# A new hand-written stream order and a new order of the first loads, in a one-core kernel of four transformer-like layers

## The chip, the cores and the metric

The kernel runs on one core of one Trainium2 chip. The metric is the device time of one execution in microseconds (us), from three runs. All arithmetic is float32. TensorE (PE in the rows) does the matrix products and transposes, VectorE (DVE) and ScalarE (ACT) move and transform what it leaves in its result banks, GpSimd (POOL) does small work for the normalisations and the residual sums, and SyncE (SP) issues every transfer between the chip's memory and the core.

## The reference, cut to what matters

There are 128 batch elements of 64 tokens with 128 features, a condition vector for each element, and a context of 64 tokens for each. Four layers follow each other:

```
layer 0:  x = x + g_sa * attend(ln(x)*(1+sc_sa)+sh_sa)        self attention, 16 heads of 8
          x = x + attend(ln(x), context)                       cross attention
          x = x + g_ff * mlp(ln(x)*(1+sc_ff)+sh_ff)            128 -> 512 -> 128, gelu
layer 1:  x = x + attend(ada_ln(x), ada_ln(context))
layer 2:  as layer 0, with ln(context) as its keys and values
layer 3:  x = x + g * out(sum_e p_e * expert_e([ln(x), evidence(x, context), anchor]))
```

The shifts, scales and gates (`sh`, `sc`, `g`) are products of silu(condition) with weights, so nothing that is modulated can start before the first modulation weights have landed.

## The kernel before, in words

The 128 elements are cut into 32 groups of 4 elements (256 tokens). A group runs through 91 named steps: `load`, `stats` (mean and variance), `normal` (normalised rows), `cols` (their transpose), `q`, `k`, `v`, `tops` (scores for the row maximum), `lows`, `scores`, `values`, `out`, `fc1`, `fc2`, the `l3_...` steps and `store`. Six streams, 0 to 5, each work through five or six groups, one after another; a stream's steps are in order, and each stream has its own tiles (`x_rows0`, `q_heads3`).

How the six streams are mixed is written out by hand in the string `SEQUENCE` (line 181): each digit is the next step of that stream, and each `f` the next of 18 set-up steps (`FOLDS`), which compute modulations, the gate rows and products of weights. `HALVES` says which half of TensorE's eight result banks each `tops` and `scores` takes. All engines walk the same list `ORDER` and each executes in that order what belongs to it, so **an instruction that waits holds up everything behind it on its engine**, whatever its stream. The string is periodic: from step 225 on, 546 steps (one group of each stream) repeat four times, before a tail of 503 steps. I call these parts the head, the four periods and the tail.

One normalisation goes through four engines: DVE sums up (`stats`, lines 1113 and 1116), POOL makes the reciprocal root (lines 707, 709, 711), DVE normalises the first 128 rows (line 1121) and ACT the other 128 (line 1279), and PE transposes (line 753).

`BY_START` lists the streams by the place of their first `stats`, and the SP program loads rows in that order. A list of weights, 12 transfers in all, is loaded with one shared semaphore `weights_in`; the only instruction that waits for it is the fold `("turn", 0)` on PE (the first transposes of line 800), and everything later on PE stands behind that. The gate rows are computed, stored to memory (`gate_store`, line 628) and loaded again for each stream, spread over the partitions (line 591). SP waits for the store to land before it goes on. The rows of streams 4 and 5 are loaded after that.

## Time and profile before

| what | value |
|---|---|
| median of 3 runs (lowest to highest) | 1828.96 us (1826.38 to 1832.3) |
| the profiled execution: its own time | 1832.71 us |
| its span, first to last instruction | 1830.8 us |
| PE busy | 1751.3 us, 96% of the span |
| DVE busy | 1554.5 us, 85% |
| ACT busy | 1484.3 us, 81% |
| POOL busy | 717.2 us, 39% |

The profiled execution took 1.9 us more than its span, and it stands 3.75 us above the median of the other runs. "Busy" is the union of an engine's instructions; an engine that is not busy waited either for another or for its own next instruction ("issue").

### The profile page before, as it was taken

How to read it: one execution, taken by the hardware profiler on the slowest of the kernel's cores; microseconds unless marked ns; L12 is line 12 of the kernel's file. 1: busy time of each engine (PE TensorE's matmuls, PEld its weight loads, DVE VectorE, ACT ScalarE, POOL GpSimd, SP SyncE). 2: the span in 40 equal slices, each digit the busy share in tenths (PEclk: the TensorE clock that was granted, in tenths of full speed). 3: DMA queues.
4: the chain of work that ended last, by engine and by line, in shares of the span. 5: the costliest groups of instructions: out<-in, count | busy, mean ns of one | idle time of the engine just before them, and what ended most of it. 6: DMA issues, size and time to landing. Idle time of an engine off the chain costs nothing.

```text
span 1830.8 us, 88396 instructions
## 1 busy us (share of the span) xinstructions
PE 1751.3 (96%) x38181; PEld 1503.1 (82%) x38181; DVE 1554.5 (85%) x3982; ACT 1484.3 (81%) x3598; POOL 717.2 (39%) x1401
## 2 busy tenths in 40 slices
PE   6889999999999999999999999999999999999998
PEld 5767788888888888888888888888888888878887
DVE  6868898888889888888988888988898898899765
ACT  4666897888888888888897888889888887786886
POOL 5323443343343344434344343434443444343341
PEclk9989999999999999999999999999999999999999
DMA  6000000000000000000000000000000000100000
GB/s 223 3 14 9 18 23 23 15 12 23 23 24 24 17 15 18 23 23 23 22 5 23 23 23 23 24 9 17 23 23 23 23 15 12 29 9 15 3 6 16
DMA packets 57841, 42.12 MB, mean 23 GB/s; under 512 B 13553, under 2 KB 56177, under 8 KB 57329
## 3 DMA queue, kind: packets, MB, share of 16 engines
q1 hardware_dynamic: 57456, 36.46, 6.8%
q8 instruction: 306, 5.01, 1.2%
q14 instruction: 79, 0.64, 0.1%
HBM read 31.99 MB, written 4.46 MB: 20 GB/s over the span
## 4 chain that ended last, share of the span: by engine, by line
PE 83%; DVE 8%; ACT 5%; issue 3%; DMA 1%; SPq 1%; DVEq 0%
PE half L1004 10%; PE half L902 8%; PE half L880 8%; PE half L921 8%; PE half L906 7%; PE half L939 6%; PE half L949 6%; PE half L1013 4%; PE half L753 4%; PE half L932 4%; PE half L867 4%; PE half L852 4%; PE half L856 3%; DVE top L1150 3%; ACT pT L1319 1%
## 5 line engine op out<-in xcount | busy, mean ns | idle before, releaser
L1150 DVE TENSOR_REDUCE top<-half 128x32 f32<-128x2048 f32 x160 | 364.5, 2278 | 48.8 <-PE half L880 47.7
L707 POOL TENSOR_TENSOR shifted<-moments,eps 128x2 f32<-128x2 f32 x256 | 50.5, 197 | 906.6 <-DVE moments L1116 906.3
L1319 ACT ACTIVATE pT<-half 128x512 f32<-128x512 f32 x640 | 330.0, 607 | 76.0 <-PE half L906 74.9
L902 PE MATMUL half<-o_rows,of_keys 32*128 32x128 f32 x5120 | 277.2, 282 | 7.8 <-issue 4.8
L906 PE MATMUL half<-q_heads,k_heads 32*128 32x128 f32 x5120 | 262.9, 271 | 0.0
L902 PEld LDWEIGHTS half<-o_rows,of_keys 32*128 32x128 f32 x5120 | 208.5, 186 | 31.1 <-issue 18.7
L1354 ACT ACTIVATE pT<-half,mod 128x64 f32<-128x64 f32 x896 | 196.5, 337 | 26.9 <-PE half L1004 25.8
L906 PEld LDWEIGHTS half<-q_heads,k_heads 32*128 32x128 f32 x5120 | 209.9, 187 | 0.1
L880 PE MATMUL half<-k_heads,q_heads 32*128 32x128 f32 x5120 | 188.0, 281 | 5.4 <-issue 2.0
L709 POOL TENSOR_TENSOR rstd<-shifted,minus_halves 128x2 f32<-128x2 f32 x256 | 182.8, 714 | 20.1
L880 PEld LDWEIGHTS half<-k_heads,q_heads 32*128 32x128 f32 x5120 | 160.4, 186 | 33.0 <-issue 15.5
L921 PE MATMUL half<-pT,v_cols 128*32 128x64 f32 x10240 | 177.7, 220 | 9.2 <-ACT pT L1319 4.6
L921 PEld LDWEIGHTS half<-pT,v_cols 128*32 128x32 f32 x10240 | 153.3, 110 | 38.7 <-issue 31.9
L1295 ACT ACTIVATE k_heads<-half,key_bias,own_head_sb 128x256 f32<-128x256 f32 x320 | 164.3, 573 | 24.3 <-PE half L856 22.7
L1142 DVE TENSOR_SCALAR q_heads<-half,b_sb,own_head_sb 128x256 f32<-128x256 f32 x320 | 156.7, 534 | 24.4 <-PE half L852 23.6
L1279 ACT ACTIVATE n_rows<-x_rows,minus,rstd 128x128 f32<-128x128 f32 x256 | 127.4, 504 | 29.6 <-POOL minus L711 27.6
L1113 DVE BATCH_NORM_STATS2 stats<-x_rows 128x6 f32<-128x128 f32 x512 | 122.4, 281 | 21.5 <-DMA x_rows<-x 18.4
L1303 ACT ACTIVATE v_cols<-half 64x256 f32<-64x256 f32 x320 | 122.7, 383 | 20.6 <-PE half L867 17.6
L1004 PE MATMUL half<-nT,w_sb 128*128 128x256 f32 x448 | 137.1, 387 | 2.1 <-issue 2.1
L939 PE MATMUL half<-nT,w_sb 128*128 128x256 f32 x512 | 133.3, 391 | 1.1 <-DVE top L1150 0.8
L1004 PE MATMUL half<-pT,w_sb 128*128 128x256 f32 x448 | 133.2, 379 | 0.7 <-issue 0.7
L949 PE MATMUL half<-w_sb,pT 128*128 128x128 f32 x1024 | 127.5, 277 | 1.0 <-DVE top L1150 0.6
(150 smaller groups left out, 3908.5 us busy)
## 6 DMA issues: line engine op xcount, KB each, us to landing
gates<-gate_store SPq DMA_DIRECT2D x128, 128.0 KB, 3.1
x_rows<-x SPq DMA_DIRECT2D x32, 128.0 KB, 2.8
c_rows<-context SPq DMA_DIRECT2D x32, 128.0 KB, 2.4
out<-n_rows SPq DMA_DIRECT2D x32, 128.0 KB, 1.9
w_sb<-weights SPq DMA_DIRECT2D x1, 1856.0 KB, 10.1
w_sb<-weights SPq DMA_DIRECT2D x2, 512.0 KB, 7.5
logit_bias<-logit_store SPq DMA_DIRECT2D x64, 1.5 KB, 3.5
row_sb<-rows SPq DMA_DIRECT2D x1, 769.5 KB, 7.7
```

The source lines that it names most:

```text
L709: nc.gpsimd.tensor_tensor(rstd[s][:, :], shifted[s][:, :], minus_halves[:, 0, :], ALU.pow).then_inc(rstd_in[s], 1)
L880: mm = nc.tensor.matmul(halves[HALF_OF[n]][:, g, tb * D:(tb + 1) * D], q_heads[s][part, tb, :, :], k_heads[s][part, tb, :, :], start=True, ...
L902: nc.tensor.matmul(halves[HALF_OF[n]][:, g, tb * D:(tb + 1) * D], of_keys[part, 2 * tb:2 * tb + 2, :], low[s][part, :], start=True, stop=F ...
L906: mm = nc.tensor.matmul(halves[HALF_OF[n]][:, g, tb * D:(tb + 1) * D], k_heads[s][part, tb, :, :], q_heads[s][part, tb, :, :], start=False ...
L921: mm = nc.tensor.matmul(dst[QUAD * g:QUAD * (g + 1), tb, :, lo, :], v_cols[s][:, at:at + QUAD], pT[s][:, g, tb, lo, :].rearrange("p (h q) ...
L939: mm = nc.tensor.matmul(dst[:, c * TOK:(c + 1) * TOK], w(layer["w1"], 0, 2 * half + c), nT[s][:, :, :], start=True, stop=True)
L949: mm = nc.tensor.matmul(dst[:, t * D:(t + 1) * D], hidden[s][:, c, t * D:(t + 1) * D], w(arg["w2"], c), start=c == 0, stop=c == 3)
L1004: mm = nc.tensor.matmul(dst[:, r * TOK:(r + 1) * TOK], weight, src[:, :, :], start=c == 0, stop=c == 1)
L1150: nc.vector.tensor_reduce(top[s][:, :].rearrange("p (g c) -> p g c", c=32)[:, :, 0:2 * GROUP], halves[HALF_OF[n]][:, :, :].rearrange("p g ...
L1295: m = nc.scalar.activation(k_heads[s][:, :, pair, :], bank4(src), ACT.Identity, scale=own_head[:, pair:pair + 1], bias=key_bias[:, n_att, ...
L1319: nc.scalar.activation(turn_cols[s][:, g, :], halves[HALF_OF[n]][:, g, :], ACT.Exp, scale=ATT_SCALE).then_inc(scores_read, 1)
L1354: m = nc.scalar.activation(dst, src[:, at], ACT.Silu, bias=mod[s][:, k, tb:tb + 1])
```

## The change

Two things change, and nothing that is computed. `SEQUENCE` and `HALVES` are other strings of the same length and with the same steps, again with a repeated block of 546 steps; the streams now begin in the order 2, 0, 1, 3, 4, 5. And the SP program loads the `x` rows of the first three streams directly behind the first modulation weights, splits the loads of `x` and `context` rows, and issues the 12 transfers of `weights_in` after the gates have been stored and loaded.

```diff
 SEQUENCE = (
-    "f023101200f0f11100f02104312f10102f31303120f23021f00023f04312f01420f11201f40310f32300f22104f22031f020"
+    "f2102012200f0f20023f01012210f23014f2311430f42102f01031f02022f10022f30231f23310f40231f11043f00240f413"
...
-                def load_rows(s):
+                def load_x(s):
                     sp.dma_start(x_rows[s][:, :, :], rows_of(x, s, 0)).then_inc(x_in[s], 16)
+
+                def load_context(s):
                     sp.dma_start(c_rows[s][:, :, :], rows_of(context, s, 0)).then_inc(c_in[s], 16)
...
                 load_weights(W_LOADS[0], 0, MOD_L0_COLS, mod_weights_in)
-                load_rows(BY_START[0])
+                for s in BY_START[:3]:
+                    load_x(s)
+                load_context(BY_START[0])
                 load_weights(W_LOADS[1], 0, L0_COLS, l0_weights_in)
+                for s in BY_START[1:3]:
+                    load_context(s)
                 load_weights(W_LOADS[0], MOD_L0_COLS, W_LOADS[0][3] - MOD_L0_COLS, later_mods_in)
-                load_rows(BY_START[1])
...
-                load_rows(BY_START[2])
-                load_weights(W_LOADS[1], L0_COLS, W_LOADS[1][3] - L0_COLS, weights_in)
-                for load in W_LOADS[2:]:
-                    load_weights(load, 0, load[3], weights_in)
-                load_rows(BY_START[3])
+                load_x(BY_START[3])
+                load_context(BY_START[3])
...
                 for s in BY_START[:4]:
                     load_gates(s, 0, 0)
+                load_weights(W_LOADS[1], L0_COLS, W_LOADS[1][3] - L0_COLS, weights_in)
+                for load in W_LOADS[2:]:
+                    load_weights(load, 0, load[3], weights_in)
                 for s in BY_START[4:]:
-                    load_rows(s)
+                    load_x(s)
+                    load_context(s)
                     load_gates(s, 0, 0)
```

The first place is the start of SP's queue, before. `pT5` and `pT4` are tiles of later streams that hold weights during set-up; the first holds the modulation weights, and `w_sb` with 1024 columns is the first layer's attention weights.

```order
L607 DMA pT5<-weights 128x768
L602 DMA x_rows0<-x 128x2x128
L603 DMA c_rows0<-context 128x2x128
L607 DMA w_sb<-weights 128x1024
L607 DMA pT5<-weights 128x1280
L602 DMA x_rows1<-x 128x2x128
L603 DMA c_rows1<-context 128x2x128
L619 DMA gates5<-rows 128x4x128
L620 DMA row_sb<-rows 128x1539
L602 DMA x_rows2<-x 128x2x128
L603 DMA c_rows2<-context 128x2x128
L607 DMA w_sb<-weights 128x3712
```

The same place in the changed kernel, and then the rows around the large weights.

```order
L609 DMA pT5<-weights 128x768
L602 DMA x_rows2<-x 128x2x128
L602 DMA x_rows0<-x 128x2x128
L602 DMA x_rows1<-x 128x2x128
L605 DMA c_rows2<-context 128x2x128
L609 DMA w_sb<-weights 128x1024
L605 DMA c_rows0<-context 128x2x128
L605 DMA c_rows1<-context 128x2x128
L609 DMA pT5<-weights 128x1280
```

```order
L630 DMA gate_store<-pT3 128x512
L591 DMA gates2<-gate_store 64x2x256 x2
L591 DMA gates0<-gate_store 64x2x256 x2
L591 DMA gates1<-gate_store 64x2x256 x2
L591 DMA gates3<-gate_store 64x2x256 x2
L609 DMA w_sb<-weights 128x3712
```

Three loads of `x` now stand together ahead of 1024 and 1280 columns of weights, and the large weights stand behind the gate store and eight gate loads; `x_rows4` follows behind all of them.

The second place is PE's queue around the first fold `turn` (the rows that transpose `w_sb` and `pT4`), before.

```order
L902 MATMUL half1<-o_rows1,of_keys 128x128 x4
L906 MATMUL half1<-q_heads1,k_heads1 128x128 x4
L852 MATMUL half0<-nT2,w_sb 128x256
L932 MATMUL half0<-w_sb,kvT0 128x128 x2
L800 MATMUL half0<-ident_sb,w_sb 128x128
L800 MATMUL half0<-ident_sb,pT4 128x128 x2
```

And in the changed kernel:

```order
L873 MATMUL half0<-w_sb,nT1 32x64 x16
L759 MATMUL half0<-ident_sb,c_rows3 128x128 x2
L927 MATMUL half0<-pT0,v_cols0 32x2x32 x32
L806 MATMUL half0<-ident_sb,w_sb 128x128
L806 MATMUL half0<-ident_sb,pT4 128x128 x2
L806 MATMUL half0<-ident_sb,w_sb 128x128
L908 MATMUL half1<-o_rows2,of_keys 128x128 x4
```

The scores of a second stream and the first `out` (line 932 before), which stood ahead of the fold, now stand behind it. On DVE, in the changed kernel, the statistics of stream 4 stand ahead of the first attention result of stream 0:

```order
L1127 TENSOR_SCALAR n_rows3<-x_rows3,moments3,rstd3 128x128
L1119 BN_STATS stats4<-x_rows4 128x6 x2
L1122 BN_AGGR moments4<-stats4 128x2 x2
L1109 BN_STATS c_stats3<-c_rows3 128x6 x2
L1111 BN_AGGR c_moments3<-c_stats3 128x2 x2
L1161 STREAM_TRANSPOSE q_heads0<-half0 128x512
```

In the kernel before, `stats4` came 19 rows behind the transpose of `q_heads0` instead of 4 rows ahead of it.

The third place is PE in the head of the changed kernel, from an `out` of stream 1 to the transposes of the rows normalised from it.

```order
L938 MATMUL half0<-w_sb,kvT1 128x128 x2
L759 MATMUL half0<-ident_sb,n_rows0 128x128 x2
L862 MATMUL half0<-cT3,w_sb 128x256
L858 MATMUL half0<-nT0,w_sb 128x256
L873 MATMUL half0<-w_sb,cT3 32x64 x16
L759 MATMUL half0<-ident_sb,n_rows1 128x128 x2
```

Only four steps stand between the two; before, the same `out` and the same transposes had `q`, `scores`, `tops`, `k`, `cols`, `values` and `lows` of other streams between them.

## Rows read from the trace of the kernel before

**Rows 1.** Page, part 1: busy time, share of the span, instructions of each engine.
```profile
PE 1751.3 (96%) x38181; PEld 1503.1 (82%) x38181; DVE 1554.5 (85%) x3982; ACT 1484.3 (81%) x3598; POOL 717.2 (39%) x1401
```
**Rows 2.** Stages: start:end us, length, busy of each engine, PE clock, DMA.
```profile
0.00:20.28 20.28, 6.18 (x26) 5.20 (x27) 8.77 (x41) 3.37 (x7) 10.62 (x38) 1.00 0.88 305
39.23:163.45 124.22, 107.37 (x2522) 89.42 (x2521) 97.70 (x224) 76.78 (x174) 36.33 (x73) 0.96 0.04 10
501.07:826.20 325.13, 321.90 (x7141) 277.33 (x7141) 288.13 (x738) 281.40 (x676) 133.28 (x258) 1.00 0.07 20
826.20:1156.80 330.60, 323.26 (x7145) 278.30 (x7141) 288.08 (x738) 281.83 (x676) 133.51 (x258) 1.00 0.08 20
1485.50:1831.00 345.50, 326.57 (x6650) 280.02 (x6646) 275.30 (x711) 266.59 (x694) 124.51 (x234) 1.00 0.05 14
```
**Rows 3.** Timeline of the start: start, length, instruction, [idle before it, releaser].
```profile
6.53 0.49 DVE L1113 BATCH_NORM_STATS2 stats<-x_rows 128x6 f32<-128x128 f32 x2 [0.29 <-DMA x_rows<-x]
14.93 0.49 DVE L1113 BATCH_NORM_STATS2 stats<-x_rows 128x6 f32<-128x128 f32 x2 [2.61 <-DMA x_rows<-x]
15.98 0.69 PE L753 MATMUL half<-ident_sb,n_rows 128*128 128x128 f32 x2 [6.70 <-DVE n_rows L1121]
16.46 1.91 PE L782 MATMUL half<-pT 128*128 128x128 f32 x8
20.28 1.06 PE L852 MATMUL half<-nT,w_sb 128*128 128x256 f32 x2
39.23 0.27 PE L800 MATMUL half<-ident_sb,w_sb 128*128 128x128 f32 x1
```
**Rows 4.** Timeline of SP's issues in the start.
```profile
8.78 0.48 SPq L607 DMA_DIRECT2D w_sb<-weights  x1
17.89 0.45 SPq L607 DMA_DIRECT2D pT<-weights  x1
19.69 0.74 SPq L628 DMA_DIRECT2D gate_store<-pT  x1
26.73 5.53 SPq L591 DMA_DIRECT2D gates<-gate_store  x8
```
**Rows 5.** Stages of the weights' landing and of two idle stretches, columns as in 2.
```profile
8.80:26.30 17.50, 9.81 (x95) 7.89 (x94) 10.25 (x37) 3.94 (x10) 5.60 (x14) 1.00 0.98 366
88.25:91.00 2.75, 0.13 (x2) 0.13 (x1) 2.33 (x5) 0.36 (x1) 0.34 (x1) 1.00 0.04 6
91.00:95.00 4.00, 4.00 (x44) 3.00 (x44) 2.24 (x5) 2.33 (x6) 0.00 (x0) 0.60 0.07 5
106.20:112.00 5.80, 5.77 (x41) 4.78 (x44) 0.99 (x2) 4.04 (x7) 0.00 (x0) 0.50 0.01 3
```
**Rows 6.** Page, part 6: transfers, count, KB each, median us from issue to landing.
```profile
out<-n_rows SPq DMA_DIRECT2D x32, 128.0 KB, 1.9
```
**Rows 7.** Timeline of PE in a steady stretch: `scores` begins, and what follows it.
```profile
704.02 0.50 PE L902 MATMUL half<-o_rows,of_keys 32*128 32x128 f32 x8
706.02 0.71 PE L1021 MATMUL half<-w_sb,pT 128*128 128x128 f32 x4
```
**Rows 8.** Page, part 5: operation xcount | busy us, mean ns of one | idle before.
```profile
L1150 DVE TENSOR_REDUCE top<-half 128x32 f32<-128x2048 f32 x160 | 364.5, 2278 | 48.8 <-PE half L880 47.7
L1319 ACT ACTIVATE pT<-half 128x512 f32<-128x512 f32 x640 | 330.0, 607 | 76.0 <-PE half L906 74.9
```
**Rows 9.** Timeline of one normalisation in the head, in time order.
```profile
142.12 0.48 DVE L1113 BATCH_NORM_STATS2 stats<-x_rows 128x6 f32<-128x128 f32 x2
144.04 0.26 POOL L711 TENSOR_SCALAR minus<-moments,rstd 128x1 f32<-128x1 f32 x1
146.01 0.49 ACT L1279 ACTIVATE n_rows<-x_rows,minus,rstd 128x128 f32<-128x128 f32 x1
```
**Rows 10.** Timeline in a period: a load that DVE, then PE, waited for.
```profile
972.21 0.49 DVE L1113 BATCH_NORM_STATS2 stats<-x_rows 128x6 f32<-128x128 f32 x2 [3.56 <-DMA x_rows<-x]
976.10 0.67 PE L852 MATMUL half<-nT,w_sb 128*128 128x256 f32 x2 [1.45 <-DVE nT L1130]
```

More of the change, by code:

```diff
@@ new lines @@
+    "20f13010f2000134140212400411023103130131203111031104230130101201000210212043012021100002013021020111"
+    "0103402410210030230100231101301112203102102044210345224310512035530420013045013512143512531104322352"
+    "1222454342513241302513002123105343315200541355104435130452114253404015210435410023045322033432535204"
+    "5203451035254124312423040052454405420555341104210352231025201325121401254134501253403055410145310453"
+    "1255532150340211314513521234021354034310353100402531534042105324502542132504154011542021500341102450"
@@ L216 @@
[L216 to L217 removed]
+    "0011000010000011110000111010011100011100000000000111111111111100000001111100000111110000011100011100"
+    "0000000001111111111111000000011111000001111100000111000111000000000001111111111111000000011111000001"
+    "1111000001110001110000000000011111111111110000000111110000011111000001100111111111110000111111110001"
+    "11110011000011100011"
 )
```

57 lines of the change are left out of this document (24 added, 33 removed).

## The prediction

> **What bounds the kernel now.** I read the page's busy shares first: PE is busy for 1751.3 us of a span of 1830.8 [rows 1], so 79.5 us is all that any order of the same work can win, before new waits. Then I cut the span into stages, to see where these 79.5 us lie [rows 2]. The stretch up to the first `q` is 20.28 us with 6.18 us of work: 14.1 us idle. From the first `turn` to the first repeated block, 124.2 us, PE is idle for 16.9 us. A period of six groups takes 325 to 331 us, and PE idles in the two shown for 3.2 and 7.3 us. The last 345.5 us hold 18.9 us of idle time. So the repeated block, which is most of the string, has little left to win; start, head and tail hold most of it. Last I read the timeline around single waits, in the order in which they fall.
>
> **The change part by part.** My reckoning is made against the profiled execution (span 1830.8, own time 1832.71 us), and the forecast is its difference, put on the median of 1828.96 us.
>
> *Three loads of x first.* The reader is to see in [rows 3] that DVE waited until 14.93 us for the third stream's `x`, because DVE does the three `stats` before it normalises stream 0, and that PE then began at 15.98 us after 6.70 us of idle time. The first `q` came at 20.28 us. In the changed queue the three loads stand directly behind the first weights, and the one behind these weights was there at 6.5 us before [rows 3]; three loads of 128 KB at 366 GB/s [rows 5] take 0.36 us each, so the last is there at about 7.3 us and DVE is through the three `stats` by 8.9 us. What is late next: PE's second transpose of context rows stands ahead of the modulation product, and those rows follow 1024 columns of weights (512 KB, 1.4 us), so about 10.1 us. From there to the first `q` stand the same steps as before: the modulation products (eight took 1.91 us there, as the `gates` products did [rows 3]), the additions and the modulating on DVE, and the `gates` products ahead of the next stream's transposes, together 5.3 us: first `q` at about 15.4 us. Gain: **4.9 us** there. The most it can be is the 6.70 us of idle time that goes; nothing less than 3 us is likely, since the `x` wait itself goes.
>
> *The large weights behind the gates.* Their widths in the order sum to 7689 columns, 3.94 MB. Before, they were issued from 8.78 to 18.3 us and the last landed 8.4 us after 17.89, at 26.3; PE needed them only at 39.23, so they had 13 us to spare [rows 3, 4]. Now: gates are added up on DVE by about 15.9 us and stored from 16.0. The store took until 26.73 before, 7.0 us, behind those weights [rows 4]. Without them I have as the nearest row a store of half the size at 1.9 us [rows 6]; I take 3.0, between 2.2 and 7.0 us, near the lower end because nothing large is queued. Eight gate loads take SP 5.53 us [rows 4], so the weights start at 24.6 us, and 3.94 MB at 366 GB/s [rows 5] is 10.8 us; with 1 us to land, `weights_in` is complete at **36.4 us** (35.0 to 40.6). The Trainium skill, in "DMA: Bandwidth & Descriptors", section "Bandwidth", gives 425 GB/s for a 16 MB load and 341 for 1 MB; by the higher figure the weights would be complete 1.5 us sooner and the sum below would be 1.5 us lower. The trace has 366 GB/s for this very traffic, and I go by it.
>
> When does PE get to `turn`? Before, 18.95 us after the first `q` [rows 3]. Counting the steps ahead of it by their start-to-start times (`scores` 2.0 us [rows 7], a projection about 0.45), the changed order has 12.1 us of PE work there instead of 13.8: one `scores` and one `out` less, a `k` and a `v` more. So PE stands at `turn` at about 32.7 us and waits **3.7 us**. Behind `turn` on PE are the second stream's `scores` and all else. For equal work: before, PE had done 12.1 us of work at 37.6 us; now it goes on at 36.4. The 4.9 us have shrunk to 1.2 us.
>
> *The clock.* PE was busy for only 0.13 of the 2.75 us up to 91 us, and its granted clock in the next 4.0 us was 0.60; in another stretch, 106.2 to 112 us, it was 0.50, which is 1.2 of 2.4 GHz [rows 5]. That costs 4.0 x 0.4 = 1.6 us and 5.8 x 0.5 = 2.9 us of the work's time. A new idle stretch of 3.7 us is longer than that first one; I take 2.2 us, between 0 and 2.9. The first stretch thus ends **1.0 us behind** the kernel before. The Trainium skill, in "TensorE: Matmul & The Clock Gate", Part 1, holds such a ramp to be under 1% of a kernel and not worth fitting; by that the 2.2 us would be left out and the sum would be 2.2 us lower.
>
> *Streams 4 and 5 behind the weights.* `x_rows4` is issued some 9.6 us after the first large weight (8.78 to 18.3 before) and lands behind them, at about 36.8 us. DVE now has `stats4` ahead of the transpose that the first `out` needs. DVE then needs 0.75 us for it, 0.9 for context statistics and 2.0 for the attention result: `out` can start at 40.5. PE in the meantime has `turn`, `scores` and `tops`, 36.4 + 0.7 + 2.0 + 1.1 = 40.2 at full clock and later at half. So it costs nothing as long as PE is itself late; were PE not held by the weights, it would cost up to 3 us.
>
> *The rest of the head.* Here I compared, for every pair of steps of one stream, how much PE work the string puts between them with what the other engines need. A normalisation needs 2.2 us from the start of DVE's sums to the end of POOL's last operation, and ACT's 0.49 us [rows 9], with the addition ahead of it about 3.3. In the head before, one of 20 pairs `out` or `fc2` to `cols` has less; after, five have (1.73, 2.20, 2.23, 2.43 and 3.20 us of work), together 5 us short, against 0.6. The order's third place shows the shortest: four small steps. The pairs `scores` to `values` improve: with 2.0 us needed for what is left of four exponentials of 607 ns [rows 8], five of 15 fall short by 2.8 us before, three by 1.3 after. From `tops` to `lows` (2.28 us of maximum [rows 8]) it is 3.5 against 4.3 us. Idle times overlap, so I take half of the difference of about 4.4 - 1.5 + 0.8: with the longer queues on DVE, **+2.5 us** (0 to +8).
>
> *The four periods.* The same count gives 3.2 us of shortage per period before and 1.2 after; most of it is `cols` to `q`, five of 48 pairs before and two after. The wait of 1.45 us at 976.10 us is one of that kind, begun by a load of the next `x` that DVE waited for [rows 10]; but the new string too leaves only 3.5 us of PE work between one `store` and the `stats` that need that load (3.1 before), so that wait can come back in another stream. I take a quarter of the difference: **-0.5 us** each, -2 in all. The bounds: -3.2 to +2 each, by the idle time that a good period has [rows 2] and by one more such wait.
>
> *The tail.* The shortage falls from 12.8 to 8.1 us, most in `scores` to `values` (seven pairs to three of 25). I take **-3 us** of the 18.9 us idle (-8 to +3).
>
> Sum: +1.0 + 2.5 - 2.0 - 3.0 = -1.5 us. **1827 us** on the median, which is no change that a measurement could tell: three runs of the kernel before differ by 0.3%, 5.5 us, and that is the bound I use.
>
> **The rivals.** *Faster* (0.35): the wait for the weights is short. If the store lands in 2.2 us and PE arrives later than I think, the wait is under 2 us and the clock stays up. That gives -3.2 us for the start instead of +1.0; with the whole shortage gone in the periods (-8) and a tail 4.7 us shorter, and the head as reckoned, -13.4: **1816 us**. For it: all counts outside the head point that way, and seven ACT table loads fewer. Against: DVE and ACT are not on PE's path most of the time, so their slack does not return one for one.
>
> *Slower* (0.27): normalisations in the head come late in the queues. In [rows 9] ACT had its input at 144.3 us and began at 146.01, as it was doing other streams' work: 1.7 us on top of the 3.3. A pair with little PE work ahead of it passes all of that on. Five pairs are short after, one before; if each loses another 1.7 us, the head costs 8.5 us more than I take, so **1836 us**. It decides from four such pairs on (4 x 1.7 = 6.8 against the 7.0 us from -1.5 to +5.5). For it: they fall in a stage where few streams are far enough to fill in. Against: they can share one wait.
>
> *The weights come at the late bound* (part of the no-change case): 40.6 us instead of 36.4 is +4.2, 1831 us. From 43.4 us on it would be a slowdown by itself.
>
> *The loads bring nothing at the start* (0.05 of the faster and no-change cases together): if the first `q` still came near 20 us because the context rows or the first weights are what PE waits for, the weights would not be waited for either, and the kernel would lose 2.5 and win 5: 1826 us.
>
> **How the numbers follow.** No change 0.38, faster 0.35, slower 0.27. The likeliest single case is the forecast, 1827 us, by itself good for 1823.5 to 1834.5. Both signs hold most of the rest, so the range goes from 1811 (the faster case with the tail's bound) to 1842 (the slower case with the weights late by part of its bound); I leave one in ten on each side.
>
> **What would show it.** Start: PE's first `q` near 15.4 us. Weights: PE's first `turn` near 36.4 us with some 3.7 us of idle time ahead of it, a granted clock below 1 behind it, and DVE waiting for `x_rows` at 36 to 37 us. Head: idle time between the first `turn` and the first period of 19 to 20 us instead of 16.9, at transposes of `n_rows`. Periods of 325 to 330 us. Tail: some 16 us idle. The forecast is wrong if PE doesn't wait at `turn`, if the periods' length moves by more than 2 us, or if stretches like the two in [rows 5] come at other places in number.

## The result, and the profile after it

The changed kernel takes 1813.22 us (median of four runs, 1810.61 to 1815.01); the kernel before took 1829.04 us in the four runs beside it (1826.38 to 1832.3). The ratio is 0.991, with a 95% interval of 0.9894 to 0.9927: faster by 0.9%, 15.8 us. The profiled execution has a span of 1812.5 us against 1830.8, 18.3 us less. Below I divide up these 18.3.

The page of the changed kernel, part 1 (busy time, share of the span, instructions), which answers to [rows 1], with the two costliest groups of part 5 under it, which answer to [rows 8]:

```profile
span 1812.5 us, 88388 instructions
PE 1742.4 (96%) x38181; PEld 1499.7 (83%) x38181; DVE 1558.8 (86%) x3982; ACT 1472.6 (81%) x3591; POOL 717.1 (40%) x1401
...
L1325 ACT ACTIVATE pT<-half 128x512 f32<-128x512 f32 x640 | 330.0, 606 | 95.5 <-PE half L912 93.3
L1156 DVE TENSOR_REDUCE top<-half 128x32 f32<-128x2048 f32 x160 | 365.0, 2282 | 36.1 <-PE half L886 33.8
```

PE executes the same 38181 matmuls, and yet its busy time is 8.9 us smaller. So half of the gain lies inside what the page calls busy, and the 79.5 us of idle time on which I founded the prediction was never "all that can be won".

To see where the time went I counted PE's matmuls in the order of the program. Both stream orders issue the same number up to the end of the head (3342), and then 7140 in each of the four periods, so a stage can be cut at the same point of the work in both. The head is the first 243 characters of the string, 225 steps of streams and the 18 set-up steps. The stages of the kernel before, cut that way (columns: start:end, length, busy of PE, PEld, DVE, ACT, POOL, PE clock, DMA share, GB/s):

```profile
39.23:186.00 146.77, 129.21 (x2956) 107.88 (x2954) 117.07 (x277) 92.53 (x209) 46.51 (x94) 0.97 0.04 9
186.00:519.50 333.50, 322.97 (x7140) 278.01 (x7140) 289.03 (x743) 281.55 (x676) 133.27 (x259) 1.00 0.07 20
519.50:844.70 325.20, 322.00 (x7140) 277.44 (x7140) 288.10 (x739) 281.52 (x675) 133.25 (x259) 1.00 0.07 20
844.70:1175.30 330.60, 323.26 (x7140) 278.30 (x7140) 288.08 (x739) 281.83 (x675) 133.51 (x259) 1.00 0.08 20
1175.30:1503.90 328.60, 322.16 (x7140) 277.47 (x7141) 287.82 (x739) 281.86 (x675) 133.16 (x258) 1.00 0.08 20
1503.90:1830.80 326.90, 308.41 (x6279) 264.29 (x6279) 258.96 (x665) 251.82 (x664) 117.63 (x219) 1.00 0.05 13
```

The same stages of the changed kernel, with its start:

```profile
0.00:15.48 15.48, 5.95 (x26) 5.04 (x26) 8.59 (x43) 3.37 (x7) 12.27 (x42) 1.00 0.78 247
15.48:39.25 23.77, 14.54 (x328) 11.65 (x329) 14.38 (x35) 10.57 (x23) 7.07 (x13) 0.92 0.78 259
39.25:189.95 150.70, 131.92 (x2989) 109.68 (x2990) 119.30 (x285) 94.71 (x208) 47.42 (x96) 0.96 0.04 10
189.95:514.20 324.25, 319.75 (x7142) 276.69 (x7142) 289.65 (x743) 277.19 (x673) 133.11 (x259) 1.00 0.07 20
514.20:841.60 327.40, 321.30 (x7144) 277.46 (x7147) 289.27 (x739) 277.31 (x673) 133.32 (x259) 1.00 0.07 20
841.60:1165.00 323.40, 320.21 (x7141) 277.26 (x7142) 289.26 (x739) 277.21 (x673) 133.52 (x259) 1.00 0.08 20
1165.00:1491.05 326.05, 320.92 (x7141) 277.21 (x7141) 289.02 (x739) 276.99 (x672) 133.04 (x259) 1.00 0.08 20
1491.05:1812.50 321.45, 307.79 (x6279) 264.69 (x6279) 259.37 (x665) 255.27 (x667) 117.39 (x219) 1.00 0.05 14
```

The reader is to see this. The start up to the first `turn` takes the same time, 39.25 against 39.23 us. The rest of the head is 3.9 us longer. The four periods take 324.25 + 327.4 + 323.4 + 326.05 = 1301.1 us instead of 1317.9: 16.8 us less. The tail with the end takes 321.45 instead of 326.9: 5.5 less. That is 3.9 - 16.8 - 5.5 = -18.4, the whole difference but for rounding. In the periods PE's busy time falls by 8.2 us (1290.4 to 1282.2) and its idle time by 8.6.

In the start, the first `q` stands at 15.48 us instead of 20.28, as the bounds of the two first stages show. What happened to it is in three timelines of the changed kernel, SP's issues, then PE and DVE (columns as in [rows 3, 4]):

```profile
16.00 0.34 SPq L630 DMA_DIRECT2D gate_store<-pT  x1
18.01 6.10 SPq L591 DMA_DIRECT2D gates<-gate_store  x8
24.15 0.59 SPq L609 DMA_DIRECT2D w_sb<-weights  x1
...
31.36 0.45 SPq L609 DMA_DIRECT2D pT<-weights  x1
31.85 0.45 SPq L602 DMA_DIRECT2D x_rows<-x  x1
```

```profile
31.79 0.42 PE L927 MATMUL half<-pT,v_cols 128*32 128x64 f32 x14 [0.19 <-issue]
39.25 0.45 PE L806 MATMUL half<-ident_sb,w_sb 128*128 128x128 f32 x1 [7.04 <-issue]
39.66 0.49 DVE L1119 BATCH_NORM_STATS2 stats<-x_rows 128x6 f32<-128x128 f32 x2 [8.89 <-DMA x_rows<-x]
```

and in the stages around them:

```profile
28.00:32.00 4.00, 3.61 (x110) 2.82 (x108) 2.66 (x7) 3.45 (x9) 3.07 (x8) 1.00 0.93 366
32.00:36.00 4.00, 0.21 (x14) 0.05 (x3) 0.00 (x0) 0.48 (x2) 0.00 (x0) 0.95 1.05 392
36.00:40.00 4.00, 0.75 (x4) 0.72 (x4) 0.34 (x2) 0.00 (x0) 0.00 (x0) 0.50 1.03 283
40.00:44.00 4.00, 4.00 (x98) 3.73 (x96) 3.16 (x12) 1.71 (x4) 2.81 (x7) 0.69 0.09 27
```

PE stops at 32.2 us and begins `turn` 7.04 us later. The row names "issue", since a wait for many transfers at once leaves no single releaser; that it is the weights is seen from their landing. Eleven of the twelve transfers had landed by 36.71 us and the last, issued at 31.36, at 39.16 us, 0.09 us ahead of `turn`. The DMA engines are full until then, and DVE's `x_rows`, which stands behind the weights, is in use only at 39.66. The granted clock is then at half (0.50) for the stage in which `turn` begins and at 0.69 in the next.

### The profile page after: what moved, and what is told of

It is laid out like the page before. It is cut to its first block, busy times and chain, and to the rows that moved or that the text cites. A ratio compares the mean times of both kernels' runs of the same rounds, so it can differ in the third digit from the quotient of the medians.

```text
span 1812.5 us, 88388 instructions
## 1 busy us (share of the span) xinstructions
PE 1742.4 (96%) x38181; PEld 1499.7 (83%) x38181; DVE 1558.8 (86%) x3982; ACT 1472.6 (81%) x3591; POOL 717.1 (40%) x1401
## 4 chain that ended last, share of the span: by engine, by line
PE 82%; DVE 10%; ACT 4%; issue 3%; DMA 1%; SPq 0%; POOL 0%; ACTq 0%; DVEq 0%
PE half L1010 10%; PE half L886 9%; PE half L908 8%; PE half L927 8%; PE half L912 7%; PE half L955 6%; PE half L945 6%; PE half L1019 4%; PE half L759 4%; PE half L873 4%; PE half L938 4%; DVE top L1156 4%; PE half L858 4%; PE half L862 3%; PE half L897 1%
## 5 line engine op out<-in xcount | busy, mean ns | idle before, releaser
L908 PEld LDWEIGHTS half<-o_rows,of_keys 32*128 32x128 f32 x5120 | 207.2, 187 | 28.9 <-issue 14.7
L1148 DVE TENSOR_SCALAR q_heads<-half,b_sb,own_head_sb 128x256 f32<-128x256 f32 x320 | 157.9, 537 | 13.3 <-PE half L858 12.2
L1309 ACT ACTIVATE v_cols<-half 64x256 f32<-64x256 f32 x320 | 122.6, 383 | 15.6 <-PE half L873 12.5
L1161 DVE STREAM_TRANSPOSE q_heads<-half 128x512 f32<-128x512 f32 x160 | 113.6, 710 | 25.2 <-PE half L927 24.4
```

The costliest lines, as they stand in the source:

```text
L908: nc.tensor.matmul(halves[HALF_OF[n]][:, g, tb * D:(tb + 1) * D], of_keys[part, 2 * tb:2 * tb + 2, :], low[s][part, :], start=True, stop=F ...
L1148: m = nc.vector.tensor_scalar(q_heads[s][:, :, lo, :], bank4(src), bias(*arg["bq"]), own_head[:, 2 + lo:3 + lo], ALU.add, ALU.mult)
```

## The experiments

The table gives, for every kernel, the first `turn`, the length of the head from there, of the four periods together and of the tail to the last matmul, all from matmuls with the same number. "Inside steps" is the waiting within the periods between two neighbouring matmuls of one step, "between steps" that from one step to the next: distances between starts of over 0.35 us, less 0.1 and 0.22 us. Some of those inside steps, of 0.4 to 0.6 us, are no waits but the half clock behind a long wait: 1.7 us of the 16.3 of before_again, 1.5 of the 16.3 of shift_before and none in before. The ratio is the time against the kernel before on the same chip.

| kernel | turn | head | periods | tail | inside steps | between steps | ratio (95%) |
|---|---|---|---|---|---|---|---|
| before | 39.23 | 146.8 | 1317.9 | 320.6 | 15.2 | 18.7 | |
| before_again | 39.10 | 145.3 | 1317.3 | 319.9 | 16.3 | 18.3 | one run |
| changed | 39.25 | 150.7 | 1301.1 | 315.8 | 8.4 | 15.6 | 0.991 (0.9894 to 0.9927) |
| periods_only | 39.33 | 146.4 | 1302.4 | 323.0 | 7.5 | 18.1 | 0.9941 (0.9927 to 0.9955) |
| tail_only | 39.94 | 144.9 | 1316.6 | 320.7 | 13.2 | 18.9 | 0.9986 (0.9972 to 1.0) |
| loads_only | 38.18 | 145.3 | 1316.6 | 319.7 | 13.3 | 19.1 | 0.9996 (0.9984 to 1.0009) |
| weights_early | 39.87 | 148.3 | 1300.8 | 315.4 | 7.6 | 15.3 | 0.9912 (0.9895 to 0.9928) |
| split_loads | 35.47 | 146.8 | 1301.1 | 316.5 | 8.6 | 14.7 | 0.9861 (0.9844 to 0.9877) |
| mix_split | 36.06 | 146.3 | 1301.3 | 317.6 | 5.6 | 18.4 | 0.9869 (0.9853 to 0.9885) |
| few_gates_before | 39.10 | 143.9 | 1314.1 | 321.9 | 13.1 | 16.1 | 0.9951 (0.9933 to 0.9969) |
| few_gates_after | 39.52 | 148.4 | 1298.6 | 314.9 | 6.5 | 14.7 | 0.9877 (0.9855 to 0.9899) |
| shift_before | 38.77 | 138.9 | 1314.8 | 321.5 | 16.3 | 15.0 | 0.9957 (0.994 to 0.9975) |
| shift_after | 44.21 | 151.0 | 1303.9 | 315.0 | 10.8 | 15.6 | 0.9951 (0.9932 to 0.9969) |
| halves_before | 39.51 | 148.7 | 1350.6 | 320.0 | 13.2 | 56.0 | 1.017 (1.0143 to 1.0197) |

### Which part of the change carries the gain

Three kernels take the change apart, and a fourth run repeats the kernel before. **periods_only** is the kernel before with one piece of both strings exchanged:

```diff
-SEQUENCE = before;  HALVES = before
+SEQUENCE = before[:243] + changed[243:2427] + before[2427:]
+HALVES   = before[:30] + changed[30:270] + before[270:]
```

> The kernel before, with its own loads, head and tail; only the four repeated periods of the stream order, and the bank string of the same stretch, are those of the changed kernel. Theory A, the new order of steps in the periods gives the gain by itself: the four periods together shrink by 15 to 18 us (from 1317.9 between the records of the first and the last matmul of them), the kernel comes to 1812 to 1815 us. Theory B, the gain in the periods comes from where the head leaves the streams and the queues when the periods begin: the four periods shrink by less than 8 us, the kernel stays above 1821 us. My forecast's pair counts alone (-2 us) would give 1827.

The periods took 1302.4 us, 15 less than in either profile of before: theory A for the periods, and with it most of the gain of the change. The kernel as a whole took 1818.82 us and gained 0.6%, less than I had expected (1812 to 1815 us), because the tail of before, now behind other periods, grew by 2.4 to 3.3 us (323.0 against 320.6 and 319.9).

**tail_only** is the counterpart: `SEQUENCE[2427:]` and `HALVES[270:]` of the changed kernel on the kernel before.

> The kernel before with only the tail of the changed stream order (and its banks). Theory A, the tail's gain is its own: the tail from the last period to the end of the matmuls falls from 320 to 320.6 us to 315 to 317.5, the waits between its steps from 14 to 9 us, the kernel by 3 to 5.5 us. Rival B, it needs the periods ahead of it (the changed periods with the tail of before took 323.0): 319 us or more and no change that can be told.

Rival B: 320.7 us, no change that can be told, though the waits between its steps fell from 14.1 to 10.8 us (inside its steps they rose from 0.7 to 2.9). The changed tail takes 315.4 to 316.5 us where the whole changed string stands ahead of it. So the tail's 5.5 us are not had by exchanging the tail alone. But part of that is the joint between the two strings. Just behind it PE waits for ACT, and the granted clock in the next 6.8 us is 0.50 (row of PE, then the stage of tail_only behind it):

```profile
1505.76 1.61 PE L880 MATMUL half<-k_heads,q_heads 32*128 32x128 f32 x33 [1.66 <-ACT v_cols L1303]
1506.50:1513.30 6.80, 6.02 (x75) 4.42 (x72) 5.90 (x7) 2.21 (x5) 0.00 (x0) 0.50 0.01 2
```

PE was busy for 6.02 us of this stage, half of which, 3.0 us, the clock cost. A second stretch at half clock (0.51 from 1677.1 to 1680.5 us) cost another 1.7, and the kernel before has neither. periods_only has the same wait for ACT at its joint (1.53 us). The two kernels with a joint thus don't tell what the changed tail is worth by itself.

**loads_only** keeps both strings of before and takes the new order of loads alone.

> The kernel before with its own stream order and banks throughout; only the order of the loads is that of the changed kernel. Theory A, the loads buy an early first q (about 15.5 instead of 20.3 us) and lose it again at the first turn: turn at 38.5 to 40 us, the four periods as before (1315 to 1320 us in sum), 1827 to 1832 us. Rival B, the loads' order changes how SP's transfers fall later too, and is part of the gain in the periods: the periods shrink by more than 5 us and the kernel comes under 1823 us.

Theory A: no change that can be told. Its `turn` came at 38.18 us, some 0.3 us earlier than I had bounded it and 1 us earlier than before, but the periods are those of before. The loads by themselves carry nothing.

**before_again** is the kernel before, profiled a second time.

> The kernel before, unchanged, profiled a second time. If the waits inside steps (PE without a next instruction for 1 to 4 us) belong to fixed places of the program, the same steps show them again and the four periods repeat within 1 us each; if they fall by chance, as a fetch of instructions that collides with other traffic would, they move to other steps and the periods differ by 2 to 5 us between the two profiles, with a sum that may differ by up to 5 us.

The sum of the periods repeats within 0.7 us, while single periods differ by up to 3.3 us (333.5 and 330.2 for the first). Of the 17 waits inside steps that the first profile has in the periods, 15 come back behind the same matmul. Four of them have the same distance to the hundredth (among them 0.98, 1.17 and 1.82 us at matmuls 23618, 26484 and 30964), others another one (1.87 and 0.81 us at 3701, 1.01 and 2.20 at 28849), and the second profile has five that the first has not. Neither "fixed" nor "by chance" was right: all lie at places from one fixed set, and whether PE stops at such a place, and for how long, varies.

### The start: two loads that both gate the first `turn`

**weights_early** moves the twelve large loads ahead of the store of the gates:

```diff
+                load_weights(W_LOADS[1], L0_COLS, W_LOADS[1][3] - L0_COLS, weights_in)
+                for load in W_LOADS[2:]:
+                    load_weights(load, 0, load[3], weights_in)
                 sp.wait_ge(v_emptied, used_by(FOLD_AT["gates", None], FOR_VECTOR))
                 sp.dma_start(gate_store, gate_rows[0:B, :]).then_inc(gates_stored, 16)
...
-                load_weights(W_LOADS[1], L0_COLS, W_LOADS[1][3] - L0_COLS, weights_in)
-                for load in W_LOADS[2:]:
-                    load_weights(load, 0, load[3], weights_in)
```

> The changed kernel, with the twelve loads of large weights issued right behind the fourth stream's rows, ahead of the wait for the gates (about 10 to 20 us instead of 24 to 31). Theory A, the late weights are what took back the early start: PE's wait of 7.0 us at the first turn shrinks to under 2 us and its half clock behind it goes, x_rows of streams 4 and 5 land by 30 us, the first turn comes at 32 to 34 us, and the gain at the end of the head is 5 to 8 us: 1805 to 1808 us. Rival B, the store of the gates waits behind the large weights, as it did before (7.0 us), and the head is bound by the normalisations anyway: the first turn is early, but the head's end moves by less than 2 us and the kernel stays at 1812 to 1814 us.

Neither had it right. The last large load was issued at 18.21 us, and still `turn` came at 39.88 us. The timeline of weights_early, one row for each engine in the order of the chain:

```profile
18.71 0.49 SPq L633 DMA_DIRECT2D gate_store<-pT  x1
27.02 5.21 SPq L591 DMA_DIRECT2D gates<-gate_store  x8
32.03 0.73 POOL L727 TENSOR_TENSOR lifted<-gates,row_sb 128x256 f32<-128x256 f32 x1 [16.66 <-DMA gates<-gate_store]
37.98 0.32 POOL L717 TENSOR_SCALAR minus<-moments,rstd 128x1 f32<-128x1 f32 x1
38.33 0.49 ACT L1285 ACTIVATE n_rows<-x_rows,minus,rstd 128x128 f32<-128x128 f32 x1 [9.22 <-POOL minus L717]
38.73 1.00 ACT L1301 ACTIVATE k_heads<-half,key_bias,own_head_sb 128x256 f32<-128x256 f32 x2
39.88 0.45 PE L806 MATMUL half<-ident_sb,w_sb 128*128 128x128 f32 x1 [8.53 <-ACT k_heads L1301]
```

The reader is to see how a transfer for one stream stops all. The store of the gates takes 8.3 us behind the large loads, POOL waits for the gates until 32.03, and the fourth stream's normalisation stands behind that in POOL's queue. ACT waits for that normalisation, with `k_heads` behind it, and PE waits for the bank that `k_heads` empties. My working of the start had no POOL in it, though the same wait was in the trace of before (POOL until 30.78 us). The weights first or the gates first: each order holds `turn` at 39 to 40 us by the other transfer.

**split_loads** gives each its turn: the largest load goes between the store and the wait for it, and the gates of three streams go ahead of the other eleven.

```diff
                 sp.dma_start(gate_store, gate_rows[0:B, :]).then_inc(gates_stored, 16)
+                load_weights(W_LOADS[1], L0_COLS, W_LOADS[1][3] - L0_COLS, weights_in)
                 sp.wait_ge(gates_stored, 16)
-                for s in BY_START[:4]:
+                for s in BY_START[:3]:
                     load_gates(s, 0, 0)
-                load_weights(W_LOADS[1], L0_COLS, W_LOADS[1][3] - L0_COLS, weights_in)
                 for load in W_LOADS[2:]:
                     load_weights(load, 0, load[3], weights_in)
+                load_gates(BY_START[3], 0, 0)
```

> The changed kernel, with the largest load of weights (1.9 MB) issued between the gates' store and the wait for it, then the gates of three streams, and then the other eleven weights. Theory A, both earlier orders hold the first turn by a transfer (the changed kernel by the weights, landed at 38.8 us; the one with the weights first by the gates, which POOL waits for until 32.0 us, with the fourth stream's normalisation behind it in POOL's queue): here the gates are at POOL by 24 to 26 us and the weights complete by 30 us, the first turn comes at 32.5 to 34.5 us, the granted clock doesn't fall to 0.5 at 36 to 40 us, and the head ends at 182 to 186 instead of 189.95: 1804 to 1809 us. Rival B, the head is bound by its normalisations whatever its start: turn early, head's end within 2 us of 188.2 to 190, 1812 to 1815 us.

Theory A, and the fastest kernel of the study: 1807.57 us (1807.22 to 1808.76), ratio 0.9861; its interval lies clear of that of the changed kernel. The head ends at 182.24 us instead of 189.95. The start was 1 us worse than I had worked out, and the clock fell all the same, which theory A had ruled out. Its timeline, and then the stage at the low clock:

```profile
27.59 0.73 POOL L728 TENSOR_TENSOR lifted<-gates,row_sb 128x256 f32<-128x256 f32 x1 [12.43 <-DMA gates<-gate_store]
35.47 0.41 PE L807 MATMUL half<-ident_sb,w_sb 128*128 128x128 f32 x1 [3.40 <-ACT k_heads L1302]
```

```profile
36.00:40.00 4.00, 4.00 (x87) 3.67 (x89) 2.85 (x11) 1.77 (x4) 2.81 (x7) 0.63 0.29 93
```

The gates came to POOL at 27.59, not by 26, and 3.4 us of the wait stayed, again through POOL and ACT.

**mix_split** has these loads, the head of before and the changed periods and tail (`before[:243] + changed[243:]`, banks alike).

> Head of the stream order from the kernel before, periods and tail from the changed kernel, loads as in split_loads. The head before took 145 to 147 us from the first turn on, the changed one 151. Theory A, heads, periods and tails add up: turn at 33 to 35, head's end at 179 to 183, periods 1301 to 1304, tail 321 to end: 1802 to 1808 us. Rival B, the junction between strings costs as it did where the changed periods met the tail of before (tail 3 us longer), and the start brings nothing: 1811 us or more.

1809.16 us (1808.98 to 1809.96), ratio 0.9869: the range of theory A, with the start slower (36.06) and the tail longer. It is not distinguishable from split_loads by the ratios' intervals. With these loads the two heads take nearly the same, 146.3 and 146.8 us, but are made of other things. The waits between steps in the head sum to 12.9 us in mix_split and 17.3 in split_loads, those inside steps to 9.6 and 4.3.

### What the gain in the periods is made of

**few_gates_before** and **few_gates_after** shrink the bursts of small packets that fall in the periods. Loads of gates after a stream's first fill 8 rows of 64 in each half, so they compute with older gates in the other rows.

```diff
+                    few = SEQ if (r, layer) == (0, 0) else 8
                     for b in range(2):
-                        sp.dma_start(gates[s][SEQ * b:SEQ * (b + 1), :, :, :].rearrange("p t n c -> p t (n c)"),
-                                     of_b[b].unsqueeze(0).broadcast_to([SEQ, 2, 2 * D])).then_inc(gates_in[s], 16)
+                        sp.dma_start(gates[s][SEQ * b:SEQ * b + few, :, :, :].rearrange("p t n c -> p t (n c)"),
+                                     of_b[b].unsqueeze(0).broadcast_to([few, 2, 2 * D])).then_inc(gates_in[s], 16)
```

> The kernel before, in which each load of gates after the first of a stream fills 8 of 64 rows per half instead of 64 (the other rows keep older gates), with all waits kept. Theory A, PE's waits without a next instruction come from fetches of instructions that queue behind these bursts of small packets: the 13 to 16 us of such waits in the four periods fall to under 6 us, the periods from 1317 to 1306 to 1311 us in sum, and the kernel to 1818 to 1823 us. Rival B, they come from something else than the transfers (the fetch itself, or the step's own work): they stay at 13 to 16 us and the kernel stays within 1827 to 1831 us.

> The changed kernel with the same small loads of gates. Theory A: its 7.6 to 8.4 us of waits without a next instruction in the periods fall to 2 to 5 us, the periods from 1301 to 1295 to 1299 us. If the fewer such waits are part of the change's gain in the periods (some 7 of 16 us), the difference between the two kernels' periods shrinks to 8 to 12 us here; if they are no part of it (rival), it stays at 15 to 17 us.

Rival B for the cause: with an eighth of the bytes the waits inside steps go from 13.3 to 16.3 us down only to 13.1, and in the changed kernel from 7.6 to 8.6 down to 6.5. The periods gain 2.1 to 3.8 us, and the whole kernels (1825.07 and 1809.66 us) 0.5% and 0.3% by their ratios, so the bursts cost something, a few us. The difference between the two kernels' periods is 15.5 us, as large as with full bursts. My theory that these loads are what makes the waits inside steps has fallen. That the waits are fetches of instructions is another matter, and is shown below.

**shift_before** and **shift_after** put 125 waits that are already met into PE's program:

```diff
                         mm.then_inc(v_filled, 1)
+                        if arg == 0:
+                            for _ in range(125):
+                                pe.wait_ge(small_in, 64)
```

> The kernel before, with 125 waits on a count that is already reached put into PE's program behind the first modulation products, where PE idles for 6.7 us. All later instructions of PE then stand half a block further along (the waits inside steps recur at distances that are multiples of about 124.5 matmuls). Theory A, a wait inside a step falls where a block of PE's instructions ends, and which steps it hits is a matter of the order's luck: the waits move to other matmuls, some 62 earlier, and their sum in the four periods changes to anything from 6 to 20 us, with the periods between 1308 and 1322. Rival B, they belong to steps or transfers: same steps, 13 to 16 us, periods 1316 to 1318. Kernel 1820 to 1836 us.

> The changed kernel with the same 125 waits. If the changed order has few waits inside steps because of where its steps fall in the blocks (A), they rise from 7.6 to 8.4 us to something nearer 15, and the periods from 1301 to 1305 to 1309; if the changed order is less open to them wherever the blocks end (B), they stay under 10 us and the periods at 1299 to 1303.

The places moved. One of the longest waits, matmul 30964, is the same in the two profiles of before; rows of before, then of before_again:

```profile
1453.79 0.76 PE L921 MATMUL half<-pT,v_cols 128*32 128x64 f32 x40
1454.48 0.48 PE L1004 MATMUL half<-nT,w_sb 128*128 128x256 f32 x1
1456.29 0.38 PE L1004 MATMUL half<-nT,w_sb 128*128 128x256 f32 x1 [1.33 <-issue]
```

```profile
1452.46 0.48 PE L1004 MATMUL half<-nT,w_sb 128*128 128x256 f32 x1
1454.27 0.38 PE L1004 MATMUL half<-nT,w_sb 128*128 128x256 f32 x1 [1.33 <-issue]
```

and in shift_before the same two matmuls follow each other without it (the row has both):

```profile
1442.72 1.10 PE L924 MATMUL half<-pT,v_cols 128*32 128x64 f32 x64
1443.75 0.70 PE L1007 MATMUL half<-nT,w_sb 128*128 128x256 f32 x2
```

Here is how such a wait is told from one for an operand. It falls between two matmuls of one step with nothing but "issue" as its releaser. Its matmul number is one of a set that is the same in both runs of the program. The numbers in it are multiples of some 124.5 apart (18017, 18142, 18266; 20382, 20508), and with waits added ahead they moved by 30 or 31 (20382 to 20351, 21378 to 21348). I had reckoned with 62; why it is half of that stays open. This is what the end of a block of fetched instructions would look like. The transfers of before from 519 to 845 us, one period, have this row (packets, MB, share of 16 engines), which is 125 of 7140 matmuls to a packet:

```profile
q8 instruction: 57, 0.93, 1.2%
```
0.93 MB in 57 packets is 16 KB each. The Trainium skill, in "Runtime: NRT & Kernel Launch", section "Instruction fetch mechanics", says that an engine's instructions are refilled in blocks of 16 KiB, 256 instructions, and that crossing a block's end is mostly hidden. The trace agrees on the size (124.5 matmuls and as many weight loads are 249). On the cost it agrees for most of the ends, and not for the up to seven of a period with waits of over 0.35 us.

The traces have the start and the length of every packet, and they settle what PE waits for. In the kernel before, for waits from the head and the periods (us from the span's start; the number is that of the matmul ahead of the wait):

| matmul | instruction packet, start to end | PE's next start | after the packet's end |
|---|---|---|---|
| 1707 | 103.83 to 104.98 | 106.23 | 1.25 |
| 3701 | 198.66 to 199.59 | 201.07 | 1.48 |
| 18017 | 857.48 to 858.91 | 860.17 | 1.26 |
| 28849 | 1354.92 to 1355.88 | 1357.12 | 1.24 |
| 30964 | 1453.99 to 1455.08 | 1456.29 | 1.21 |

It is so without exception: the 14 profiles have 182 distances of over 0.6 us inside steps from `turn` on, and each ends 1.20 to 1.59 us after the end of an instruction packet. At the 284 block ends of the kernel before without a wait, the last packet had ended 3.4 us earlier in the median, and at 26 of them less than 1.6 us, just in time. So these waits are fetches that came late. A packet starts 0.9 us in the median after PE has passed the block end before the one at which it is needed, so only about one block is fetched ahead. PE takes 5.4 us in the median for a block. Of the blocks that it was through in under 5 us, 125 in the kernel before and 117 in the changed one, 17 and 10 ended in a distance of over 0.35 us; of the longer ones 2 of 177 and 4 of 185 did. The new order has hardly fewer short blocks, so what makes a fetch late enough to be seen is not told by this.

The changed kernel has such waits too, at other steps (its row):

```profile
833.64 0.53 PE L927 MATMUL half<-pT,v_cols 128*32 128x64 f32 x20 [1.44 <-issue]
```

As to the sums, theory A was right on the places, and on the size only by half for the changed kernel. The changed kernel's rose from 7.6 to 8.6 us to 10.8, the periods from 1301 to 1303.9; those of before stayed at 16.3 us and the periods came down to 1314.8. With the blocks moved, the order still gains, 10.9 us instead of 16.2. The surprise was outside the periods: the head of shift_before took 138.9 us instead of 145.3 to 146.8, with 1.5 us of waits inside steps instead of 8.8 to 9.3, and the kernel got 0.4% faster by instructions that do nothing. The two long waits of the head, up to 91 and 106 us in the kernel before, are such fetches, and they are the waits behind which the half clock stands in [rows 5]; in shift_before the granted clock of the whole head is 1.00, against 0.97. In shift_after the added waits take 4.55 us of PE's path, which has no idle time left there to hide them: the first `q` came at 20.77 us, the gates were stored from 21.31 instead of 16.00, and `turn` came at 44.21.

As whole kernels the two are level, at 0.9957 and 0.9951 of the kernel before. From shift_before to shift_after the `turn` is 5.4 us later and the head 12.1 us longer, and the periods and the tail are 10.9 and 6.5 us shorter. The gain in the periods outlasts a moved block, and the 0.9% of the whole kernel does not.

**halves_before** is the changed kernel with `HALVES[30:270]`, the banks in the periods, of before.

> The changed kernel, with only the string of bank uses in the four periods from the kernel before. Theory A, the order of steps makes the gain and the banks little: periods 1300 to 1305 us, kernel within 3 us of the changed one. Rival B, with other banks PE waits for a bank to be emptied: the work inside steps grows by the 5 us that it lost from before to after or more, periods 1306 to 1315.

Rival B, by far more than I had put on it: the periods took 1350.6 us, 49.5 more, and the kernel is 1.7% slower than before. Rows of the page of halves_before, part 5, and the same two groups of the changed kernel:

```profile
L908 PE MATMUL half<-o_rows,of_keys 32*128 32x128 f32 x5120 | 278.9, 285 | 23.8 <-ACT pT L1325 8.9
L886 PE MATMUL half<-k_heads,q_heads 32*128 32x128 f32 x5120 | 187.9, 282 | 27.5 <-ACT pT L1360 8.5
```

```profile
L908 PE MATMUL half<-o_rows,of_keys 32*128 32x128 f32 x5120 | 275.5, 282 | 7.5 <-issue 4.4
L886 PE MATMUL half<-k_heads,q_heads 32*128 32x128 f32 x5120 | 188.8, 282 | 7.7 <-DVE kvT L1142 4.3
```

PE's idle time ahead of these two lines goes from 15.2 to 51.3 us, and the releaser named first is now ACT (8.9 and 8.5 us), which reads the banks that PE is to fill again. Over the four periods PE is idle for 56.4 us instead of 18.9, which is 37.5 of the 49.5 us; the other 12.0 are busy time, with a mean granted clock of 0.99 instead of 1.00. The bank string is part of the order: a new order with the old banks is slower than either kernel. The old order with the new banks was not run.

## Why the prediction was right and where it was wrong

The range (1811 to 1842) held the time, but the case I called likeliest, no change that can be told, did not come. The "faster" rival did, with another sum than I gave it. The forecast of 1827 us was 14 us off, and the range held the time by its width and not by the working. By my own signs (periods that move by more than 2 us) the forecast was wrong.

**The start.** First `q`: 15.4 forecast, 15.48 measured. The store: issued 16.0, as forecast, and 2.0 us long, not 3.0. The first large load was issued at 24.15 (24.6 forecast). The last one landed at 39.16 us, not 36.4, within my bound of 40.6. Two things were off. The large weights were not alone on the DMA engines: from 24.15 to 38.8 us these moved 5.0 MB, at 341 GB/s against the 366 I took, of which the weights are 3.94; the rest is gates and rows. And issuing the twelve loads took to 31.8, 7.7 us, so the last one was asked for late. PE stopped at 32.2 (32.7 forecast) and so waited 7.0 us, not 3.7. At the first `turn` the two kernels were level (39.25 and 39.23).

**The clock.** A half clock was forecast behind the wait and came, 0.50 in the stage from 36 to 40 us. I had taken 2.2 us for it. By the two stages it is 1.6: 0.31 of the 4 us after 40 is 1.2 us, and half of the 0.75 busy us before that 0.4. The trace speaks for counting such a term, against the rule of the Trainium skill that I had weighed ("TensorE: Matmul & The Clock Gate", Part 1); the rule's bound, under 1% of a kernel, holds, but 1.6 us is a tenth of the effect looked for.

**The rest of the head.** I had +1.0 for the start and +2.5 for the normalisations, +3.5 at the head's end; measured +3.95. The term for the waits was near: those between steps in the head sum to 17.0 to 17.3 us in the four kernels with the changed head and no added waits or small loads, and to 12.8 to 14.7 in the six with the head of before and no added waits or small loads, some 3.3 us more (17.1 against 13.9 in the mean). Two terms that I did not have stand beside it. Waits inside steps are 1.8 us fewer in the changed kernel (7.3 against 9.1, the mean of the two profiles of before), and in split_loads 4.8 fewer (4.3), so there the head is no longer than before. Both sums hold some 2 us of half clock, and some of the rest is where fetches fall. And the start was level, not 1.0 behind, while what follows `turn`, the low clock and the late streams, cost some 2.4 more: 3.9 - 3.3 + 1.8 = 2.4 us, of which the clock is 1.6.

**The periods.** This is the step that failed: "I take a quarter of the difference: -0.5 us each". It was -4.2 us each, -16.8 in all, and outside my own bound of -3.2 each. Two things were wrong in it. First, the bound came from the idle time of a good period, as though busy time were fixed; half of the gain was inside busy time. Second, the count of short pairs knew one kind of wait only, that for an operand, and not the fetch of instructions. By the table, waits inside steps give 6.7 us of the gain (mean of before, before_again and loads_only against changed, weights_early and split_loads: 14.9 and 8.2), waits between steps of over 0.35 us give 3.5 (18.7 and 15.2), and 6 us are many smaller distances. The second part is not the string's own: in periods_only and mix_split, the changed periods behind the old head, it is 18.1 and 18.4 us, nearly as before, while the waits inside steps are 7.5 and 5.6 and the smaller distances again 6 to 7 us less. With the blocks shifted the same parts are 5.5, -0.6 and 6.0, so the smaller ones are the steady part. The kind that I did count is seen: ahead of `q` the kernel before has seven distances between starts of 0.61 to 1.83 us in the periods, the changed kernel none over 0.5, and what is over the usual 0.22 us falls by 1.3 us a period. That is over twice what I took for all kinds; ahead of other steps the waits grew. Why one string leaves fewer of the smaller distances stays open.

**The tail.** -3 forecast, -5.5 measured, within its bound (-8). The tail of the changed string brought nothing without its periods (tail_only); the wait at the joint and the half clock behind it have a part in that.

**The rivals.** "Faster" was reckoned with a short wait at the start, periods at -8 and a tail 4.7 better, 1816. The time came near (1813), while its first leg did not happen and its second was twice as large. "Slower", from normalisations that come late in the head, has its mechanism in the 3.3 us of added waits there, and did not get its further 8.5. "The weights come at the late bound" nearly happened, 39 us of 40.6. "The loads bring nothing at the start" is half true in a way I had not seen: they bring 4.8 us at `q` and lose all of it at `turn`. The row of POOL in the trace of before, its wait for the gates, would have shown me that putting the weights first again does not free `turn` either.

## What to carry to other kernels

An early start is worth what the next gate lets through: list every transfer that something in the first stretch waits for, on every engine's queue (here weights on PE and gates on POOL), and see that neither is issued wholly behind the other. Splitting them gave 0.5% on top of a new order that had given 0.9%.

Idle time in the profile is not a floor for what an order can win, since small distances between matmuls are counted as busy. Compare two orders of the same work by the time of the same numbered matmul.

This order, 0.9% better, hung on where blocks of instructions end and on its bank string. Test such a result with some idle instructions added in a slack place: here they moved the whole kernels by 0.4% one way and the other, and what stayed of the order was 10.9 us in the periods.

## What the runs showed of the hardware

- PE stops at some of a fixed set of places, about 124.5 matmuls (with their weight loads) apart. The distances between starts there go up to 2.2 us in the periods and 3.8 in the head. In the kernel before the waits inside steps sum to 15 to 16 us in the periods and 9 in the head. 125 waits added ahead moved the places by 30 or 31 matmuls and shortened the head by 6.4 to 7.9 us.
- They are fetches of instructions: all 182 distances of over 0.6 us inside steps in the 14 profiles end 1.20 to 1.59 us after the end of an instruction packet of 16 KB, and such a packet starts 0.9 us in the median after PE has passed the block end before.
- Cutting the bytes of the gate loads to an eighth shortened the periods by 2.1 to 3.8 us. So transfers have a share in what PE loses, and a small one. The waits inside steps fell little, from 13.3 to 16.3 us to 13.1 and from 7.6 to 8.6 us to 6.5.
- A 256 KB store behind nothing large took 2.0 us, and 8.3 us behind 3.9 MB of queued loads.
